# Turning the softmax offsets on TensorE and spreading them with one transfer and a selector, in place of VectorE and eight transfers

## The reference

```python
x = x + cross_attention(layernorm(x), ctx, ctx, k_length)   # x, ctx (16, 256, 512)
x = x + moe(layernorm(x), Wg, w1, w2)                       # 8 experts, top 2, capacity 1280, 512 -> 2048 -> 512
# cross_attention, heads of 32 channels:
attn = jnp.einsum('bhdq,bhdk->bhqk', qh, kh)                # (16, 8, 512, 512)
attn = softmax(s * attn)                                    # s = SCALE * log(k_length)
out  = jnp.einsum('bhqk,bhdk->bhdq', attn, vh)
```

## Time and profile before

| | |
|---|---|
| median of 3 runs | 2195.29 us (2194.59 to 2198.80) |
| the profiled execution | 2198.80 us, span 2197.1 us |
| PE / DVE / ACT / POOL busy | 96% / 46% / 32% / 22% of the span |
| DMA | 216.70 MB, mean 99 GB/s; 40295 of 184460 packets under 512 B |
| first stage | about 0 to 679 us; experts from 690 us |

### The profile page before, as it was taken

The page is one execution under the profiler, slowest core; times in us unless marked ns, Lnnn a source line. Parts: engine busy times, 40 slices in busy tenths (PEclk is TensorE's granted clock), DMA queues, the critical chain, the costliest instruction groups (busy, mean ns, idle before and its releaser), DMA issues. The chain is left out here.

```text
span 2197.1 us, 26958 instructions
## 1 busy us (share of the span) xinstructions
PE 2117.3 (96%) x10098; PEld 1509.5 (69%) x10098; DVE 1017.1 (46%) x1903; ACT 713.2 (32%) x1214; POOL 476.6 (22%) x598
## 2 busy tenths in 40 slices
PE   4999999999995999999999999999999999999997
PEld 2444454444445888878888888887888788888776
DVE  5777888878854434224423423332432342343211
ACT  1666666666652222112212212211321221131110
POOL 3334444343422210210301111031030102101101
PEclk9999999999996999999999999999999999999999
DMA  9877777777725344222613522522351252342101
GB/s 147 161 164 148 180 158 186 164 175 165 153 96 153 107 92 125 51 40 79 136 20 71 128 53 40 126 66 40 99 113 21 60 125 47 59 116 39 14 9 19
DMA packets 184460, 216.70 MB, mean 99 GB/s; under 512 B 40295, under 2 KB 111983, under 8 KB 184304
## 3 DMA queue, kind: packets, MB, share of 16 engines
q1 hardware_dynamic: 154692, 173.28, 34.3%
q0 software_dynamic: 22240, 37.92, 8.9%
q10 hardware_dynamic: 7372, 3.42, 0.7%
HBM read 113.93 MB, written 68.29 MB: 83 GB/s over the span
## 5 line engine op out<-in xcount | busy, mean ns | idle before, releaser
L1251 DVE SCALAR_TENSOR_TENSOR hlo<-ps_h,hhi 128x512 fp32r<-128x512 f32 x256 | 177.0, 692 | 934.4 <-ACT hhi L1129 934.4
L1129 ACT ACTIVATE hhi<-ps_h 128x512 fp32r<-128x512 f32 x256 | 152.8, 597 | 1128.5 <-PE ps_h L1392 1128.5
L1411 PE MATMUL ps_y<-w2hi,hlo 128*128 128x512 f32 x1024 | 404.5, 395 | 1.8 <-issue 1.8
L1390 PE MATMUL ps_h<-xhi,w1hi 128*128 128x512 f32 x1024 | 404.5, 395 | 1.3 <-PEq L976 1.3
L1409 PE MATMUL ps_y<-w2hi,hhi 128*128 128x512 f32 x1024 | 404.3, 395 | 0.7 <-DVE hlo L1251 0.7
L1391 PE MATMUL ps_h<-xlo,w1hi 128*128 128x512 f32 x1024 | 404.8, 395 | 0.0
L1410 PE MATMUL ps_y<-w2lo,hhi 128*128 128x512 f32 x1024 | 404.6, 395 | 0.0
L1392 PE MATMUL ps_h<-xhi,w1lo 128*128 128x512 f32 x1024 | 404.4, 395 | 0.0
L564 DVE TENSOR_REDUCE nmax<-ps_s 128x1 f32<-128x512 f32 x512 | 335.5, 681 | 122.3 <-PE ps_s L773 118.4
L430 ACT ACTIVATE probs<-ps_t 128x512 f32<-128x512 f32 x512 | 278.5, 603 | 193.6 <-PE ps_t L783 153.5
L1390 PEld LDWEIGHTS ps_h<-xhi,w1hi 128*128 128x128 f32 x1024 | 192.3, 188 | 49.0 <-issue 2.6
(11 more groups left out here) (158 smaller groups left out, 1998.1 us busy)
## 6 DMA issues: line engine op xcount, KB each, us to landing
raw<-in_L_ffn_w SPq DMA_DIRECT2D x128, 512.0 KB, 4.8
qst<-qhi SPq DMA_DIRECT2D x64, 256.0 KB, 5.8
xin<-dispatched SPq DMA_DIRECT2D x60, 256.0 KB, 5.8
kst<-khi SPq DMA_DIRECT2D x52, 256.0 KB, 6.2
xt<-in_x SPq DMA_DIRECT2D x32, 256.0 KB, 3.0
ct<-in_ctx SPq DMA_DIRECT2D x32, 256.0 KB, 4.3
qst<-qlo SPq DMA_DIRECT2D x32, 256.0 KB, 7.1
xres<-in_x SPq DMA_DIRECT2D x32, 256.0 KB, 4.3
```

What stands on the lines that cost most here:

```text
L1129: nc.scalar.activation(hhi[k % 2][:], ps_h[k % 3][:], ACT.Relu).then_inc(hhi_ready, 1)
L1251: nc.vector.scalar_tensor_tensor(hlo[k % 2][:], ps_h[k % 3][:], 0.0, hhi[k % 2][:].bitcast(F32), ALU.max, ALU.subtract).then_inc(h_ready, 1)
L1390: nc.tensor.matmul(to, w1hi[:, c, fs], xhi[n % 2][:, c, :], start=(c == 0), stop=False)
L1411: done = nc.tensor.matmul(ps_y[b][:], hlo[k % 2][:, bs], w2hi[:, f, :], start=False, stop=(f == NF - 1))
```

## The change

The maxima are turned on PE: four transposes of 128x32 into one T bank (a new turn `"m"`, placed in c1 after T(1,1)). ACT copies the bank to `mrow` (32x512) right after the exponential of T(1,1). SP then issues one transfer that writes eight rows of `mrow` to rows 96 to 103 of `qst`, each repeated for the four heads. The key side holds, in place of ones, a selector `sel` that is 1 only where the row belongs to the head: DVE zeroes it (128x2048) at the start, POOL writes ones with two `affine_select`, and ACT copies it to the five key buffers with five transfers in slot 0. The T matmul has 104 rows in place of 98. The transpose on DVE, the eight transfers and POOL's five memsets go.

```diff
@@ bank_turns
+                if i == 1 and c == 1 and live(s - 1):
+                    t_turn["m", s - 1] = len(t_turn) + 1
@@ tiles
+        sel = probs[2]
-        nturn = [sb(f"nturn{i}", [P, NC4, HD]) for i in range(2)]
+        mrow = sb("mrow", [HD, D], F32R)
@@ sync
-                    sp.wait_ge(nmax_turned, g + 1)
-                    for a in range(NC4):
-                        for part in range(2):
-                            first = HD * a + HPG * part
-                            sp.dma_start(qst[g % KR][STACK + part:STACK + part + 1, :, :].bitcast(F32).rearrange(
-                                         "o h (i a j) -> o h i a j", i=NC4, a=NC4)[:, :, :, a, :],
-                                         nturn[g % 2][first:first + HPG, :, :]).then_inc(mrow_ld[g % KR], 16)
+                    sp.wait_ge(t_free, t_turn["m", g])
+                    sp.dma_start(qst[g % KR][STACK:STACK + MROWS, :, :].bitcast(F32),
+                                 mrow[0:MROWS, :].bitcast(F32).unsqueeze(1).to_broadcast([MROWS, HPG, D])
+                                 ).then_inc(mrow_ld[g % KR], 16)
@@ gpsimd, slot 0
+                    pool.wait_ge(dve_const, 1)
+                    for part in range(2):
+                        if part:
+                            pool.wait_ge(sel_made, 1)
+                        nc.gpsimd.affine_select(out=sel[STACK:P], in_=sel[STACK:P], compare_op=ALU.not_equal, fill=1.0,
+                                                base=-HPG * part, pattern=[[-1, HPG], [0, D]],
+                                                channel_multiplier=1).then_inc(sel_made, 1)
+                    pool.wait_ge(sel_made, 2)
@@ gpsimd, each slot
                     if s >= 2:
-                        pool.wait_ge(nmax_turned, s - 1)
+                        pool.wait_ge(t_done, t_turn["m", s - 2])
...
-                if 0 <= s < KR:
-                    pool.wait_ge(nmax_ready, s + 1)
-                    nc.gpsimd.memset(kst[s][STACK:STACK + 2].bitcast(F32), 1.0).then_inc(ones_made, 1)
-                    pool.wait_ge(ones_made, s + 1)
@@ scalar, after the exponential of step i
+                        if i == 1 and c == 1 and live(s - 1):
+                            g = s - 1
+                            k = t_turn["m", g]
+                            act.wait_ge(t_done, k)
+                            if g >= 1:
+                                act.wait_ge(mrow_ld[(g - 1) % KR], 16 * turns(g - 1, KR))
+                            nc.scalar.activation(mrow[:], ps_t[(k - 1) % 3][0:HD, :], ACT.Copy).then_inc(t_free, 1)
@@ scalar, end of slot 0
+                    act.wait_ge(sel_made, 2)
+                    for i in range(KR):
+                        act.dma_start(kst[i][STACK:STACK + MROWS].bitcast(F32), sel[STACK:STACK + MROWS]
+                                      ).then_inc(sel_st, 16)
@@ vector, start
             dve.wait_ge(klen_ld, 16)
+            nc.vector.memset(sel[:], 0.0).then_inc(dve_const, 1)
             nc.vector.tensor_copy(klen_f[:], klen_i[:]).then_inc(dve_const, 1)
@@ vector, c1
-                        if (c, i) == (1, 0) and live(s - 1):
-                            g = s - 1
-                            dve.wait_ge(nmax_ready, g + 1)
-                            if g >= 2:
-                                dve.wait_ge(mrow_ld[(g - 2) % KR], (16 * 2 * NC4) * turns(g - 2, KR))
-                            nc.vector.transpose(nturn[g % 2][:], nmax_hl[g % 2][:]).then_inc(nmax_turned, 1)
@@ tensor
-                                pe.wait_ge(mrow_ld[g % KR], (16 * 2 * NC4) * turns(g, KR))
-                                if g < KR:
-                                    pe.wait_ge(ones_made, g + 1)
+                                pe.wait_ge(mrow_ld[g % KR], 16 * turns(g, KR))
+                                if g == 0:
+                                    pe.wait_ge(sel_st, 16 * KR)
-                            nc.tensor.matmul(bank[:], kst[g % KR][0:STACK + 2, i, cols],
-                                             qst[g % KR][0:STACK + 2, i, :], start=True, stop=True).then_inc(t_done, 1)
+                            nc.tensor.matmul(bank[:], kst[g % KR][0:STACK + MROWS, i, cols],
+                                             qst[g % KR][0:STACK + MROWS, i, :], start=True, stop=True).then_inc(t_done, 1)
+                        if i == 1 and c == 1 and live(s - 1):
+                            g = s - 1
+                            pe.wait_ge(nmax_ready, g + 1)
+                            bank = t_bank(t_turn["m", g])
+                            for q in range(NC4):
+                                done = nc.tensor.transpose(bank[0:HD, P * q:P * q + P], nmax_hl[g % 2][:, q, :], ident[:])
+                            done.then_inc(t_done, 1)
```

More of the change, by code:

```diff
@@ L183, in attention_and_dispatch @@
         sharp_ln = sem("sharp_ln")
-        ones_made = sem("ones_made")
+        sel_made = sem("sel_made")
+        sel_st = sem("sel_st")
         fill_st = sem("fill_st")
@@ L198, in attention_and_dispatch @@
         t_done = sem("t_done"); t_free = sem("t_free")
-        nmax_done = sem("nmax_done"); nmax_hi = sem("nmax_hi"); nmax_ready = sem("nmax_ready"); nmax_turned = sem("nmax_turned")
+        nmax_done = sem("nmax_done"); nmax_hi = sem("nmax_hi"); nmax_ready = sem("nmax_ready")
         pv_done = sem("pv_done"); o_saved = sem("o_saved"); l_saved = sem("l_saved")
@@ L363, in _ @@
                     if g == 0:
-                        pool.wait_ge(dve_const, 2)
+                        pool.wait_ge(dve_const, 3)
                     nc.gpsimd.tensor_tensor(st1[g % 2][:, 10:11], st1[g % 2][:, 9:10], sharp[:, g // 2:g // 2 + 1],
@@ L395, in _ @@
                     pool.wait_ge(nmax_hi, s + 1)
-                    nc.gpsimd.tensor_tensor(nmax_hl[s % 2][:, :, HPG:MROWS].bitcast(F32R), nmax[s % 2][:],
+                    nc.gpsimd.tensor_tensor(nmax_hl[s % 2][:, :, HPG:MROWS], nmax[s % 2][:],
                                             nmax_hl[s % 2][:, :, 0:HPG], ALU.subtract).then_inc(nmax_ready, 1)
-                if 0 <= s < KR:
-                    pool.wait_ge(nmax_ready, s + 1)
-                    nc.gpsimd.memset(kst[s][STACK:STACK + 2].bitcast(F32), 1.0).then_inc(ones_made, 1)
-                    pool.wait_ge(ones_made, s + 1)
             for r in range(RING):
@@ L419, in _ @@
                     if s == -2 and c == 0:
-                        act.wait_ge(dve_const, 1)
+                        act.wait_ge(dve_const, 2)
                         nc.scalar.activation(sharp[:], klen_f[:], ACT.Ln).then_inc(sharp_ln, 1)
@@ L490, in _ @@
                     if s == 1:
-                        act.wait_ge(dve_const, 4)
+                        act.wait_ge(dve_const, 5)
                     for n in (2 * s - 2, 2 * s - 1):
@@ L534, in _ @@
                     nc.vector.memset(fill[:], 0.0).then_inc(dve_const, 1)
-                    dve.wait_ge(dve_const, 3)
+                    dve.wait_ge(dve_const, 4)
                     nc.vector.memset(fill[:, IDCOL:IDCOL + 1].bitcast(I32), S).then_inc(dve_const, 1)
@@ L540, in _ @@
                     nc.vector.tensor_copy(e_f[:], e_i[:]).then_inc(dve_const, 1)
-                    dve.wait_ge(dve_const, 5)
+                    dve.wait_ge(dve_const, 6)
                     nc.vector.tensor_scalar(e_row0[:], e_f[:], float(CAP), None, ALU.mult)
@@ L544, in _ @@
                     nc.vector.memset(before[0][:, 0, :], 0.0).then_inc(dve_const, 1)
-                    dve.wait_ge(dve_const, 6)
+                    dve.wait_ge(dve_const, 7)
                     nc.vector.tensor_copy(before[0][0:1, 0, :], e_row0[0:1, :]).then_inc(rt["start"], 1)
@@ L552, in _ @@
                         nc.vector.tensor_scalar(sharp[:], sharp[:], SCALE, None, ALU.mult).then_inc(dve_const, 1)
-                        dve.wait_ge(dve_const, 2)
+                        dve.wait_ge(dve_const, 3)
                     q_scaled(s + 2)
```

## The result

The changed kernel took 2215.6 us (median of four runs, 2215.07 to 2218.86) against 2197.1 for the kernel before beside it (2194.59 to 2199.87): ratio 1.0090, interval 1.0075 to 1.0104. It is slower, as forecast, but by 18.5 us and not by 11.9. The profiled executions agree: 2217.91 against 2198.80, spans 2216.2 and 2197.1, so +19.1.

The account below looks back on a forecast made before the run. PE, nearly always at work, was taken as the bound, with waits in c1, c2 of pair slots and the start. Slots +8.1 and start +3.8 gave +11.9, median 2207.2 us; range 2198 to 2216; +9 to +14 had chance 0.50.

Parts of the forecast that it names:

- c1, +0.48: Block c1: T(1,3) waits for T(1,1)'s exponential, +0.48 us per slot without routing, +0.42 in pair slots.
- c2 of pair slots, -0.57: Block c2 of slots with routing: `hot` and `picked` on DVE no longer collide with POOL, -0.57 us each.
- Slot 2, +0.9,: Slot 2, where matmuls run at half pace: the transposes add 2 x 0.47 = +0.9 us.
- The memset: Start: DVE's zeroing of 128x2048 ahead of its queue delays the first slots by 1.9 us.
- POOL's selects: Start: POOL's two selects over 2048 elements run while it would wait for DVE's statistics, so cost nothing.
- The wait for the first maxima: Start: the 1.25 us wait shrinks with one transfer for eight; taken as -0.7, between -1.25 and +0.5.
- The five selector transfers: Start, DMA engines full: 0.32 MB at 124 GB/s adds 2.6 us, bounds 0 and 8.8.
- dear selector transfers: Rival at the start: the selector's transfers cost 8.8 in place of 2.6 us; +18.1, 2213.4 us; chance 0.08.
- The collision stays: Rival in c2 of pair slots: DVE and POOL still collide, 6.3 us more; +18.2, 2213.5 us; chance 0.12.
- Small transfers were the brake: Rival: the maxima's 128-byte pieces held up other transfers, whose waits would return; +8.8, 2204.1 us; chance 0.12.
- SP's 4.8 us are worth nothing in the middle: Steady slots: SP issues one transfer for eight, some 4.8 us less per slot, with no gain in time.

Follow-up runs that it names:

- the order experiment: Kernel with two rows and no selector, ACT copying the sums after T(1,0)'s exponential and sending them after the copy of `mrow`: 2205.57 us, ratio 1.0020.
- its own experiment: Changed kernel with DVE's zeroing of the selector moved behind the first group's scaling: one execution, span 2215.3 us.
- four attempts to shorten c1 or c2: ACT's sums later, in the kernel before (0.9993) and with two rows (1.0020); POOL's residual ahead of `klo`, kernel before (1.0016); two rows, turn in S bank (1.0049).
- POOL's other order: Kernel before with POOL's residual placed ahead of `klo`, nothing else changed: 2204.11 us, ratio 1.0016.

## Why the prediction was right or wrong

**c1, +0.48.** Right in size: 5.34 to 5.39 in the slots from 3 to 31 but slot 10, which is +0.47 to +0.52 in most slots without routing and +0.40 to +0.45 in nearly all pair slots, for which I had 0.42. The ring's three banks and ACT's late first exponential set it, as the order experiment shows (0.38 back with the transposes in place). PE's own work with the transposes is not 4.84 but about 5.0 (4.96 to 5.00 with ACT out of the way), so it would not quite have fitted: some 0.13 of the 0.48 would have come without the ring. One detail was wrong: I had T(1,3) wait for the exponential of T(1,1); it is T(1,2) that waits, for that of T(1,0), and PE's own pace carries it on. Both come to the same sum. A count was off too, without effect: 26 and not 27 of the 29 slots lie within 0.1 of 4.87 before (not 5, 9 and 24).

**c2 of pair slots, -0.57.** Right, mechanism and size. `hot` starts 0.18 sooner behind its block's start and `klo` 0.47 later, for my 0.22 and 0.49. **Slot 2, +0.9,** was wrong: from its first T to the end of c2 it is 0.9 shorter (11.65 against 12.59), for a reason that no term had.

**The memset.** 1.76 for 1.9; its own experiment gives 2.2, with 0.57 of an earlier load in it. **POOL's selects** (3.97 us for two) were hidden, as argued. **The wait for the first maxima** shrank by 1.0 where I took 0.7.

**The step that failed is the term of the start, "The five selector transfers, 5 x 64 KB, stand in the full stretch: 0.32 MB at 124 GB/s is +2.6".** I priced them by bytes at the rate of transfers into many partitions. In a row of eight that form measured 1.7 each and not 0.5; alone in the kernel before they move slot 2 by 5.4, and taking them out of the changed kernel returns 4.4 there. That is inside the bounds of 0 to 8.8, but I had taken the lower part of them from a row of bytes, when source and destination have eight partitions.

**And it has a second part, that no step had.** I ended the account of the start at slot 2, as if a queue that is late were then late no more. A full DMA queue behaved here like a debt. It was still there in slots 3 and 4 (share 1.07 at 78 to 84, where the kernel before has 0.38), loads that landed in 2.8 to 5.4 us took 11.7 to 12.9, and the first small transfer with a reader at once behind it, the sums to `l_wide`, came 5.9 us late for DVE. With the clock behind the pause this is 8.1 us, more than the transfers cost at slot 2. Without the selector transfers 11.9 of the 14.5 us up to slot 4 are gone, so both parts hang on them. But they are not enough for the second: alone in the kernel before they make 3.1 of it and no such stall. What they need beside them, and how much of the sums' wait is owed to the two 264 KB transfers ahead of them in ACT's queue, no run shows.

Of the rivals, dear selector transfers (2213.4) had the right mechanism, with the wrong account: 8.8 at once, where it was 5 at once and 8 later, so that its number is near is in part luck. "The collision stays" came as near (2213.5) by luck alone, since the collision is gone. "Small transfers were the brake" is refuted: the pieces of 128 bytes cost no more than SP's issue of them; of the waits it wanted back, 1.0 of the 1.25 came, but with the pieces gone and no selector PE still waits 2.38 of the 2.64 for `qlo`. "SP's 4.8 us are worth nothing in the middle" held: c0 and c3 of the steady slots take 3.93 and 4.99 (5.26 in pair slots) with one transfer, with two and with eight.

**The maxima's transfer.** In a row of eight it takes 1.56 us of the queue, with half of the engines' time (0.5 to 0.8 us of all 16 per slot by the lines of q1), which I had not priced. In the steady slots it is covered; the kernels with eight rows (and ACT's selector) and with two differ by 0.0013 in their ratios, 2.9 us, of which the memset is about 2.

**What stays open.** PE's turn alone, without selector and memset, gives 1.0005, no measurable difference: it gains 2.1 up to slot 4 (94.32 against 96.42) and 0.57 in c2 of pair slots, and loses 0.48 in c1 of every slot. But none of four attempts to shorten c1 or c2 brought time, since c3 of even slots then grew. What the traces show is that DVE and ACT there both start late on matmuls that PE had run on time, and that this goes with the phase of the slot: the first of POOL's four scatters, which fall into even slots, mostly starts 1.5 to 1.7 before S(3,0) in the kernels that don't show it, and 1.8 to 1.9 (2.8 with the residual first) in those that do, there in some slots and not in others; and with the maxima's transfer doubled it came at 1.7 too, so the phase is not all of it. What holds both engines back was not found.

## What to carry to other kernels

Price a DMA by the partitions that it spans as well as by its bytes: one from eight into eight partitions cost as much as two or more of the same size from 32 into 32. When the queues are full, follow the debt past the first reader, to the next small transfer on which an engine waits at once: that one paid more here than the bulk transfers. A further turn in a ring of banks can cost one reader's step in every round (here most of 0.48 us in a block), even if the engine that fills the ring has nearly the time. And half a microsecond won in one block is not yet won: in four kernels here a later block gave it back.

## What the runs showed of the hardware

In a row of eight, a transfer of 64 KB from eight into eight partitions takes 1.6 to 1.7 us of the DMA queue, at a DMA share of 0.47 to 0.51, and 1.04 to 1.10 of SP to issue, against 0.8 or less and 0.63 into 32 partitions. Where DVE (two SBUF inputs) met POOL, it met it in full: 0.18 became 1.0 to 1.27. And the granted clock fell behind a pause of PE of 4.41 us, but also behind two of 0.37 and 0.46 (POOL's other order, c3 of slot 16): 0.50 in the four microseconds from 337, the lower level of 1.2 GHz, with the `weighted` matmuls at 1.94 in place of 1.07.
